# First attention stage: the value projections of the first block go ahead of its score maxima, with new step orders

## The reference, cut to what matters

```python
qkv = x @ w_qkv + b_qkv
q, k, v = jnp.split(qkv, 3, axis=-1)          # 16 heads of 16
a = jnp.einsum('bhsd,bhtd->bhst', q, k)
a = (a + causal_mask) / np.sqrt(HEAD_DIM)
a = jax.nn.softmax(a, axis=-1)
z = jnp.einsum('bhst,bhtd->bhsd', a, v)
return z @ w_out + b_out
```

## Time and profile before

| what | value |
|---|---|
| three executions | 1783.2, 1787.78, 1791.49 us |
| the profiled execution | 1787.27 us |
| its span, first to last instruction | 1785.7 us |
| PE busy | 95% of the span |
| DVE, ACT, POOL busy | 64%, 56%, 49% |
| mean granted TensorE clock | 0.963 of full |

### The profile page before, as it was taken

How to read it: one execution, slowest core, us unless ns; L and a number is a source line. 1 busy time by engine, 2 the same in 40 slices (tenths; PEclk the granted TensorE clock), 3 DMA queues, 4 the chain that set the end, 5 groups by cost and what they waited for, 6 DMA issues and landing times.

```text
span 1785.7 us, 42024 instructions
## 1 busy us (share of the span) xinstructions
PE 1704.7 (95%) x13984; PEld 1305.2 (73%) x13984; DVE 1150.5 (64%) x2853; ACT 997.9 (56%) x1927; POOL 866.6 (49%) x886
## 2 busy tenths in 40 slices
PE   5999999999799999999989999899999999999997
PEld 3667566666477777777768888677777777778886
DVE  6678777787876676766643443876766776545554
ACT  2556576566545565555554555565555655655443
POOL 3343344434644665644643333556445656445453
PEclk7898898989989999999999999999999999999999
DMA  7454554544211011110023122101110010222221
GB/s 224 132 134 121 147 165 142 144 124 122 61 48 37 0 35 35 35 35 23 2 83 118 62 67 72 60 14 35 35 35 6 29 35 23 84 70 84 94 82 48
DMA packets 102327, 129.64 MB, mean 73 GB/s; under 512 B 15834, under 2 KB 70788, under 8 KB 102276
## 3 DMA queue, kind: packets, MB, share of 16 engines
q1 hardware_dynamic: 96084, 106.44, 20.5%
q0 software_dynamic: 6192, 22.55, 3.6%
HBM read 82.55 MB, written 46.15 MB: 72 GB/s over the span
## 4 chain that ended last, share of the span: by engine, by line
PE 81%; DVE 6%; DMA 4%; issue 3%; ACT 3%; POOL 1%; SPq 1%; DVEq 0%; POOLq 0%; ACTq 0%
PE b L1210 8%; PE d L1104 6%; PE b L1235 6%; PE d L1105 5%; PE d L1106 5%; PE d L631 3%; PE d L1151 3%; PE b L676 3%; PE d L1176 3%; PE b L704 3%; PE d L1623 2%; PE d L1625 2%; PE d L1624 2%; PE b L1250 2%; DMA a_K<-qk_parts 2%
## 5 line engine op out<-in xcount | busy, mean ns | idle before, releaser
L454 ACT ACTIVATE a_PT<-b 128x384 f32<-128x384 f32 (+1 forms) x384 | 183.6, 523 | 151.3 <-PE b L676 99.5
L491 DVE TENSOR_REDUCE a_negm<-d 128x2 f32<-128x256 f32 (+3 forms) x256 | 201.1, 814 | 67.1 <-PE d L637 65.3
L907 POOL TENSOR_TENSOR l_t<-l_t,l_t 128x512 f32<-128x512 f32 x128 | 165.0, 1297 | 113.4 <-DVE l_t L1059 113.3
L1077 DVE CUSTOM_DVE_ANT_0 d<-d,window 128x256 f32<-128x256 f32 (+1 forms) x512 | 184.4, 422 | 24.9 <-PE d L1176 24.6
L1476 POOL TENSOR_TENSOR m_hid_lo<-m_hid,m_hid_hi 128x512 fp32r<-128x512 f32 x80 | 103.3, 1301 | 161.6 <-ACT m_hid_hi L1537 161.5
L991 ACT ACTIVATE l_PT<-b 128x512 f32<-128x512 f32 (+1 forms) x256 | 125.3, 542 | 97.0 <-PE b L1218 95.0
L921 POOL TENSOR_TENSOR l_PS<-l_PT 128x768 f32<-128x768 f32 x64 | 117.6, 1838 | 111.4 <-ACT l_PT L991 111.4
L1104 PE MATMUL d<-w,l_xt 128*128 128x512 f32 x384 | 165.6, 431 | 4.8 <-DVE l_t L1059 4.7
L379 POOL TENSOR_SCALAR_AFFINE_SELECT a_PT<-a_PT 128x512 f32<-128x512 f32 x128 | 80.4, 656 | 180.3 <-ACT a_PT L454 179.6
L1105 PE MATMUL d<-w,l_xt 128*128 128x512 f32 x384 | 152.6, 398 | 0.0
L1106 PE MATMUL d<-w,l_xt 128*128 128x512 f32 x384 | 152.3, 397 | 0.0
(11 more groups left out here) (222 smaller groups left out, 4885.5 us busy)
## 6 DMA issues: line engine op xcount, KB each, us to landing
qk_parts<-a_qk_hi SPq DMA_DIRECT2D x64, 256.0 KB, 3.4
a_Q<-qk_parts SPq DMA_DIRECT2D x64, 192.0 KB, 3.7
a_K<-qk_parts SPq DMA_DIRECT2D x64, 192.0 KB, 4.6
qk_parts<-a_qk_lo SPq DMA_DIRECT2D x32, 256.0 KB, 4.0
xin<-after_attn SPq DMA_DIRECT2D x32, 256.0 KB, 3.1
m_xr<-after_attn SPq DMA_DIRECT2D x16, 512.0 KB, 3.9
after_attn<-rows_out POOLq DMA_DIRECT2D x14, 512.0 KB, 5.4
xin<-in_L_attn_x SPq DMA_DIRECT2D x8, 512.0 KB, 3.3
```

The source lines that it names most:

```text
L454: nc.scalar.activation(PT[:, p // PG % 2, 2 * (p % PG) + hh, QOFF[t]:QOFF[t] + nq], SC[hh][:, 0:nq], ACT.Exp, scale=AD ** -0.5).then_inc(e ...
L491: dve.tensor_reduce(negm[:, q, 2 * p:2 * p + 2], MX[i % 2][:, :, 0:nk], AX.X, ALU.max, negate=True).then_inc(max_done, 1)
L907: pool.tensor_tensor(t1[:, par, w, :], t1[:, par, w, :], t2[:, par, w, :], ALU.add)\
L1077: m = dve.tensor_tensor_reduce(out=o, in0=o, in1=mask, scale=-1.0, scalar=-NEG, op0=ALU.add, op1=ALU.min, accum_out=negm[:, q + t, p // 2, ...
```

## The change

In `OPENING`, the four value projections follow the four query and key projections on PE and DVE, ahead of `f_sm:0`; `nw:0` moves from behind `f_qk:0` to behind `f_load:1` and `f_sm:5`; `f_load:2` comes ahead of `f_mt:0` on SP, and `f_load:3` behind it; `f_mt:0` comes one `f_sm` earlier. The waits of the opening change with the turns of the two front banks: `f_v:2` waits for all four evictions instead of the second row of maxima, and `f_mt:0` waits for the third value eviction instead of the fourth projection's. The `f_x` of the loop gets one more wait, on the second row of maxima of the block before.

In `STEPS`, engine by engine, the order on PE from `f_x` on was

```diff
     STEPS = parse("""
-        f_xe:0 f_x:0 sm:27 st:8 sm:28 xr:0 mt:2 st:9 f_qe:0 f_qk:0 f_qk:1 f_qe:1 st:10 sm:29 ms:2 f_qk:2 ms:3
-        f_load:0 sm:30 f_load:1 st:11 sm:31 f_qe:2 pv:0 st:12 z0:0 mt:3 f_qe:3 z1:0 f_qk:3 st:13 pv:1 f_sm:0
-        st:14 f_sm:1 f_sm:2 st:15 f_sm:3 st:16 f_sm:4 st:17 f_sm:5 f_sm:6 st:18 f_sm:7 st:19 ms:4 f_sm:8 st:20
-        z2:0 f_sm:9 f_sm:10 st:21 f_sm:11 ms:5 z0:1 ms:6 f_sm:12 st:22 z1:1 f_mt:0 f_sm:13 z3:0 st:23 z2:1
-        pv:2 z0:2 f_sm:14 ms:7 z1:2 f_st:0 f_ms:0 f_load:2 f_load:3 f_sm:15 z0:3 pv:3 z3:1 z2:2 f_st:1 f_v:0
+        f_x:0 f_xe:0 sm:27 xr:0 st:8 mt:2 f_qk:0 f_qk:1 f_qe:0 f_qe:1 f_load:0 f_qk:2 ms:2 st:9 sm:28 f_load:1
+        sm:29 sm:30 st:10 ms:3 sm:31 f_qe:2 pv:0 st:11 mt:3 z0:0 st:12 z1:0 f_qk:3 st:13 f_qe:3 z2:0 pv:1 z0:1
+        st:14 f_sm:0 ms:4 f_sm:1 st:15 f_load:2 f_sm:2 f_sm:3 st:16 f_sm:4 z1:1 z3:0 st:17 f_sm:5 f_sm:6 st:18
+        ms:5 f_sm:7 st:19 f_sm:8 st:20 f_sm:9 ms:6 f_sm:10 f_mt:0 st:21 f_sm:11 f_sm:12 ms:7 st:22 f_sm:13
+        z2:1 f_sm:14 z0:2 st:23 pv:2 z1:2 f_sm:15 f_sm:16 z0:3 z3:1 f_st:0 z2:2 pv:3 f_load:3 f_v:0 z1:3
...
     OPENING = parse("""
-        f_x:0 f_qk:0 nw:0 f_xe:0 f_qk:1 f_qk:2 f_qe:0 f_qk:3 f_qe:1 f_load:0 f_sm:0 f_sm:1 f_sm:2 f_sm:3
-        f_qe:2 f_sm:4 f_sm:5 f_sm:6 f_qe:3 f_sm:7 f_load:1 f_load:3 f_sm:8 f_sm:9 f_sm:10 f_mt:0 f_ms:0
-        f_sm:11 f_sm:12 f_v:0 f_sm:13 f_sm:14 f_st:0 f_sm:15 f_load:2 f_st:1 f_sm:16 f_sm:17 f_st:2 f_sm:18
-        f_sm:19 f_mt:1 f_sm:20 f_st:3 f_sm:21 f_v:1 f_st:4 f_v:2 f_st:5 f_sm:22 f_sm:23 f_v:3 f_ms:1 f_st:6
-        f_sm:24 f_sm:25 f_st:7 f_sm:26""")
+        f_x:0 f_qk:0 f_xe:0 f_qk:1 f_qk:2 f_qk:3 f_v:0 f_v:1 f_v:2 f_qe:0 f_qe:1 f_v:3 f_sm:0 f_load:0 f_qe:2
+        f_sm:1 f_qe:3 f_ms:0 f_sm:2 f_sm:3 f_load:1 f_sm:4 f_sm:5 nw:0 f_sm:6 f_load:2 f_sm:7 f_sm:8 f_sm:9
+        f_mt:0 f_sm:10 f_sm:11 f_sm:12 f_sm:13 f_st:0 f_sm:14 f_sm:15 f_load:3 f_st:1 f_sm:16 f_st:2 f_sm:17
+        f_sm:18 f_st:3 f_sm:19 f_mt:1 f_sm:20 f_st:4 f_sm:21 f_sm:22 f_st:5 f_sm:23 f_st:6 f_ms:1 f_sm:24
+        f_sm:25 f_sm:26 f_st:7""")
...
                     if not isinstance(b, int) and h == 0:
+                        pe.wait_ge(mrow_done, b * AG - 2)
                         pe.wait_ge(v_done, b * TB - 1)
...
                 elif i == 2:
-                    pe.wait_ge(mrow_done, b * AG + 2)
+                    if isinstance(b, int):
+                        pe.wait_ge(front_free, NE)
+                    else:
+                        pe.wait_ge(mrow_done, b * AG + 2)
...
                 if i == 0:
-                    pe.wait_ge(front_free, b * NE + NE)
+                    if isinstance(b, int):
+                        pe.wait_ge(v_done, 3)
+                    else:
+                        pe.wait_ge(front_free, b * NE + NE)
```

More of the change, by code:

```diff
@@ L264, in first_attention @@
     STEPS = parse("""
-        f_xe:0 f_x:0 sm:27 st:8 sm:28 xr:0 mt:2 st:9 f_qe:0 f_qk:0 f_qk:1 f_qe:1 st:10 sm:29 ms:2 f_qk:2 ms:3
-        f_load:0 sm:30 f_load:1 st:11 sm:31 f_qe:2 pv:0 st:12 z0:0 mt:3 f_qe:3 z1:0 f_qk:3 st:13 pv:1 f_sm:0
-        st:14 f_sm:1 f_sm:2 st:15 f_sm:3 st:16 f_sm:4 st:17 f_sm:5 f_sm:6 st:18 f_sm:7 st:19 ms:4 f_sm:8 st:20
-        z2:0 f_sm:9 f_sm:10 st:21 f_sm:11 ms:5 z0:1 ms:6 f_sm:12 st:22 z1:1 f_mt:0 f_sm:13 z3:0 st:23 z2:1
-        pv:2 z0:2 f_sm:14 ms:7 z1:2 f_st:0 f_ms:0 f_load:2 f_load:3 f_sm:15 z0:3 pv:3 z3:1 z2:2 f_st:1 f_v:0
-        z1:3 f_st:2 z3:2 f_mt:1 f_sm:16 z2:3 f_sm:17 f_st:3 f_v:1 f_sm:18 f_v:2 z3:3 f_sm:19 out:0 out:1
-        f_sm:20 f_st:4 out:2 out:3 f_st:5 f_ms:1 f_sm:21 f_sm:22 f_st:6 f_sm:23 f_st:7 end:0 f_sm:24 f_v:3
+        f_x:0 f_xe:0 sm:27 xr:0 st:8 mt:2 f_qk:0 f_qk:1 f_qe:0 f_qe:1 f_load:0 f_qk:2 ms:2 st:9 sm:28 f_load:1
[3 more added lines that the diff above has]
+        z2:1 f_sm:14 z0:2 st:23 pv:2 z1:2 f_sm:15 f_sm:16 z0:3 z3:1 f_st:0 z2:2 pv:3 f_load:3 f_v:0 z1:3
+        f_st:1 z3:2 f_mt:1 f_sm:17 z2:3 f_v:1 f_st:2 f_sm:18 z3:3 f_v:2 f_st:3 f_sm:19 out:0 f_st:4 f_sm:20
+        out:1 out:2 out:3 f_st:5 f_sm:21 f_ms:0 f_ms:1 f_sm:22 f_st:6 f_sm:23 f_st:7 f_sm:24 f_v:3 end:0
         f_sm:25 f_sm:26""")
```

## The result

| | median | range | profiled execution | its span | mean clock |
|---|---|---|---|---|---|
| before | 1786.12 us | 1783.2 to 1791.49 (6 runs) | 1787.27 | 1785.7 | 0.963 |
| after | 1803.95 us | 1798.55 to 1811.31 (6 runs) | 1807.09 | 1805.6 | 0.955 |

The ratio is 1.0098, 95% interval 1.0076 to 1.012. The forecast was 1783.7 us, with 1796 as its upper end, so the result lies outside the range, on the side of rival B.

The account below looks back on a forecast made before the run. PE (TensorE), busy 95% of the span, was taken as the bound. From the profiled 1787.27 us, opening -1.0, reordering 0 and low stretches -3.1 gave 1783.2, against the median 1783.7 us; range 1771 to 1796.

Parts of the forecast that it names:

- rival B: Loop, ahead of `sm:30`: 1 us idle drops the clock, `pv:0` takes 4.24 instead of 2.36 us; 1799 us, chance 0.17.
- The opening: First block: value projections moved into PE's 7.88 us wait, `f_x` at 53.0; -1.0 us in all, ends -5 and +2.
- the wait ahead of `f_sm:0`: Loop: PE's wait for the stacked keys, mean 0.98 us in six iterations, was to go.
- the reordering itself: Loop, seven iterations: the new order of steps apart from the low clock, taken as 0, ends -5 and +5.
- the term that decides: Low-clock stretches in the loop: one fewer of the five, -3.1 us.
- The wait was forecast at 1.0 us: Ahead of `sm:30`: reduction of `sm:28` queued behind `xr`; 1.0 us idle in place of 0.29 ahead of `sm:31`.
- Its bound of 1 us: Rival B decides from where the addition ends over 1 us behind PE's arrival at `sm:30`.
- The forecast booked `z1:1` at 0.4 us: Mix behind `f_sm:0`: DVE gets `z1:1`, 0.4 us, between the reductions, making the mix thinner for PE.
- Rival A: Iterations 1 to 6: most low stretches go if the wait tips the clock; 12 to 16 us, 1768 to 1775; chance 0.23.
- The contention claim: POOL's low parts beside DVE's `xr` addition: shared SBUF interfaces slow the second to 2.25 us; the 0.9 us stay.
- a reader of the order alone: Moving `xr` on DVE: such a reader would book -0.9 us in six iterations, 5 us in all.
- The rule cited from the Trainium skill: Clock falls from many small waits between groups; by it none of the five stretches need go, alone giving 1786 us.

Follow-up runs that it names:

- e3: Kernel before with only the new opening and its waits: 1787.09 us, 0.9998 of before.
- e5: Kernel after with DVE's addition of `xr` moved behind `z1:0` (the late addition): 1776.87 us, 0.9933; a second time 1777.14 us, 0.995.
- e2: Kernel before with DVE's addition of `xr` moved ahead of the reduction of `sm:28`: 1786.29 us, 1.0003.
- e1: Kernel after with DVE's addition of `xr` put back behind the reduction of `sm:28`: 1797.11 us, 1.0062.
- e17: Kernel after with only `z1:1` one maximum later, behind `f_sm:5`: 1783.59 us, 0.9978.
- e8: Kernel after with `f_qk:2` behind `sm:29` on PE, the addition of `xr` still ahead of `sm:28`: 1802.25 us, 1.0076.
- e13: Kernel after with DVE's addition of `xr` moved from ahead of `sm:28` to behind `sm:29`: 1791.92 us, 1.0026.
- e15: e13 with `z1:1` one maximum later, behind `f_sm:5`: 1779.7 us, 0.9956.
- e16: e5 with `z1:1` one maximum later, behind `f_sm:5`, as a control: 1777.64 us, 0.9969.
- e6: Kernel before with DVE's addition of `xr` moved behind `z1:0`: 1793.65 us, 1.0029.
- e14: e5 with `st:14` put back behind `f_sm:0`: 1778.34 us, 0.9958.
- e9: e5 with `z1:1` put back behind `st:22`: 1802.58 us, 1.0097.
- e4: Kernel after with the opening of before, so the new loop order alone: 1804.55 us, 1.0101.
- e10: e5 with SP's `f_load:0` put behind `f_load:1`, so that the stacks land later: 1822.46 us, 1.0208.

## Why the prediction was wrong

**What held.** The opening went as worked out: the value projections lie between 17.6 and 21.6 us at no cost, the clock stays at 0.50 until 58 us, `f_st:0` waits 1.0 us, `f_x` starts at 54.1 (forecast 53.0). One row of this sum was misread: 61.0 us is the end of `f_qk:0`; `f_qk:1` starts at 60.85 and ends near 62.4. Alone it is worth nothing (e3), inside the bounds given. In the loop, PE reaches `sm:30` 8.3 us behind `f_x`, as forecast; the stacks land before PE needs them, and the wait ahead of `f_sm:0` is gone. In a clean iteration the reordering itself is worth -0.3 us (52.1 in e5 for 52.4 before), close to the 0 that was taken.

**The step that failed** is the one called "the term that decides": "I take one stretch fewer of the five: -3.1". It priced only stretches that could go away. The change made two new waits in front of thin work, and falls follow both.

First, around `pv:0`. The wait was forecast at 1.0 us and taken as only that; it is 1.56. PE's arrival was right and the addition was late: it started 7.46 us behind `f_x` instead of 6.98 and took 2.03 us instead of 1.90. Rival B had this mechanism and gave it 0.17, because "`pv:0` and `f_qk:3` are dense and close by". But `pv:0` itself runs at the low clock: +1.3 us of wait net of the 0.25 that stays in any order, +1.4 us of slower `pv:0`, 2.7 us in each of six iterations (54.8 for 52.1). B counted four such falls; there are six. Its bound of 1 us fits the rows and is not isolated by them: behind 0.78 us there is no fall (e2, in the old order on PE), behind 1.09 us in two parts (e1) and behind 1.56 us there is one; but one of five waits of 1.55 us in e17 and one of six of 1.69 us in e8 have none.

Second, in the mix. The forecast booked `z1:1` at 0.4 us of DVE between reductions, and took as reason against a gain that the mix gets thinner. The row was right for the multiplication alone, but it was put beside POOL's mask, where it takes 0.86. What follows is a 0.46 us wait of PE and a fall in five of six iterations, 3.3 us each (58.1 for 54.8). Moving this one step by one maximum gives 12 us (e13 to e15) or 20 us (after to e17). No rival named this.

Set against the kernel before, the two do not weigh the same. Iterations 1 to 5 took 277.1 us: five times 52.4, and 15.1 for four falls in the mix. Now they take 287.4 us: five times 52.1, five times 2.7 around `pv:0`, and 13.4 for four falls in the mix. In iteration 6, clean before, 2.7 and 4.4 us are added. So of the 18.6 us the falls around `pv:0` are 16.2 and the mixes 2.7, where the forecast had -3.1; the join adds 3.9, the opening with iteration 0 takes off 2.7 and the order itself 1.5. The wait of 0.46 us is less a new loss than the reason why the mixes did not get better, as they do in e17.

**How the two add up.** Neither wait: 1777 to 1780 (e5, e15, e16). The first alone: 1784 (e17). The second alone: 1792 (e13). Both: 1804. The late addition of e5 removed both at once, since POOL's and DVE's work also lie otherwise in its mix; its 27 us are not the price of the blocked queue alone. Of the 27, taking away the wait of 0.46 us first gives 20 (e17, which has fewer falls around `pv:0` as well), and taking away the wait of 1.56 us first gives 12 (after to e13). With the short wait gone the time is 1783.6, which is the number forecast; that comes about by other terms (almost no fall in the mixes, a fall around most `pv:0`) and counts for nothing.

**Rival A** had a true core: in e5 and e17 most falls in the mix go once the waits ahead of them are gone. (Its 1768 is not reached by its own terms: 12 to 16 us off 1786.8 is 1771 to 1775.) But it looked at the wait ahead of `f_sm:0`, which was removed and not replaced, and in the kernel after the clock falls in five of six mixes without it.

**The contention claim** was half wrong. That DVE's addition and POOL's work beside it lengthen each other is shown, but which of them pays differs. With POOL idle the addition takes 1.22 us and two low parts take 2.53 (e6). Before, the addition took 1.90 and the low parts 3.51. After, the low parts start earlier, keep their 2.53, and the addition takes 2.03; so the sentence that the 0.9 us of POOL stay is wrong as well. In e5 the addition starts first and keeps its 1.22, and the two masks take 2.28 instead of 1.23. The addition in e6, then the masks in e5, iteration 3:

```profile
243.84 1.22 DVE L502 TENSOR_TENSOR a_xr<-a_xr,a_bo 128x1024 f32<-128x1024 f32 x1
```

```profile
231.04 2.28 POOL L378 TENSOR_SCALAR_AFFINE_SELECT a_PT<-a_PT 128x512 f32<-128x512 f32 x2 [1.93 <-ACT a_PT L453]
```

The Trainium skill, GPSIMD Engine Reference, section Specifications, names this contention, and the trace agrees; it covers the multiplication of `z1:1` as well. But the 0.9 us are not on the chain to `f_sm:0`: with the overlap gone (e6) the first load is issued 12.3 us behind `f_x` instead of 12.4, and the wait ahead of `f_sm:0` does not shrink. So a reader of the order alone would have booked 5 us that aren't there to be had.

**On the size of waits.** The rule cited from the Trainium skill, TensorE: Matmul & The Clock Gate, section "A second HAM failure mode: psum-queue depth-cycling", puts falls down to frequent small idles between groups of matmuls. e15 and e17 agree in that a small wait is enough: without the one of 0.46 us the mixes have four falls instead of six, and one instead of five. How many such waits it takes no run here counts, and the falls around `pv:0` follow one wait of 1.56 us. The forecast used the rule only to argue that nothing would change.

**What stays open.** Two or three falls in six iterations remain in e5, e14 and e16 with no wait over 0.3 us in front of them, and e15 has four, three of them beside waits of 0.2 to 0.5 us for the row of maxima or an exponential; e9 has five. What brings them was not found. A wait alone does not decide it: the join's wait of 0.98 us stands in the same place in all 19 traces, and within 2 us behind it the clock falls in eight of them (the kernel after, e3, e4, e5, e6, e9, e10, e15) and stays up in the other eleven, the kernel before and e17 among them. So no run here puts the join's 3.9 of the 18.6 us down to the new order. Nor is it shown why the wait of 0.46 us is followed by a fall in five iterations and not in the sixth, or why the kernel before stands waits of 0.8 to 1.4 us ahead of `f_sm:0` in one iteration and not in another. That the late addition removes the 0.46 us wait by shifting POOL's work is read from the trace and was not isolated. The falls were counted in one trace of each kernel, two for e5, and the traced execution is not always a middle one: 1785.31 us for a median of 1779.7 in e15, 1771.77 for 1777.64 in e16.

## What to carry to other kernels

When a step that waits for a transfer or for another engine moves up in an in-order queue, look at what is queued behind it and who needs that; here one DVE step in front of two reductions (after to e13) and one beside a mask, with a reduction behind it (e13 to e15), cost 12 us each. Price a moved DVE instruction with what POOL does beside it at its new place, not with its median. And where PE's work is thin, price a new wait of even half a microsecond with the clock as well: here the waits themselves cost less than what ran at half clock behind them.

## What was not expected of the hardware

A wait of 0.46 us, in work that keeps PE busy for most of the time, was followed by 10 to 14 us at 1.2 GHz in five iterations of six, and the edit that removes it made the kernel 1.1% faster (1803.95 to 1783.59 us). Behind a wait of 0.98 us in the join, which the change leaves as it is, the clock fell within 2 us in eight of 19 traces and stayed up in eleven. A 128x256 multiplication on DVE took 0.86 us beside POOL's mask and 0.41 us alone; beside the mask with another offset it took 0.48 us (e5). Waits of 3.2 to 4.0 us ahead of the mix brought 20.5 us at 1.2 GHz each (e10).
